# Orders of single instructions on every engine, with the rotary sine products and two decay products on GpSimd

## What is computed

```python
x = x + 0.5 * ffn0(layernorm(x))    # 8 experts, top 2, gated, and one shared expert
x = x + attn0(layernorm(x))         # 32 heads, no softmax: q (k v), then a group norm
x = x + 0.5 * ffn0(layernorm(x))
x = x + 0.5 * ffn1(layernorm(x))    # 8 experts, top 1, layernorm inside, gelu
x = x + attn1(layernorm(x))         # 8 heads, rotary q and k, gated running state
x = x + 0.5 * ffn1(layernorm(x))
```

```python
rope(x) = concat(x1 * c - x2 * s, x1 * s + x2 * c)      # x1, x2: halves of a head of 16
M = M * f_t + g_t * scale * (k_t outer v_t);  y_t = (q_t M) * o_t
```

## Time and profile before

| | us |
|---|---|
| median of three runs | 1223.96 (1218.2 to 1229.26) |
| span of the profiled execution | 1611.3 |
| PE busy in it | 1208.2 |
| DVE busy | 1037.9 |
| ACT busy | 881.7 |
| POOL busy | 645.2 |
| mean granted TensorE clock | 0.851 of full |

### The profile page before, as it was taken

One profiled execution on the slowest core, in us unless ns is written; L12 is line 12 of the kernel. 1 busy time (PEld: TensorE's weight loads), 2 busy tenths in 40 slices (PEclk: granted clock), 3 DMA queues, 4 the chain that ended last, 5 costly groups with the idle time before them and its releaser, 6 DMA issues.

```text
span 1611.3 us, 37336 instructions
## 1 busy us (share of the span) xinstructions
PE 1208.2 (75%) x14084; PEld 950.7 (59%) x14113; DVE 1037.9 (64%) x3441; ACT 881.7 (55%) x1505; POOL 645.2 (40%) x679
## 2 busy tenths in 40 slices
PE   3745767567766778767666766799989897989997
PEld 2423545455555666555554645677877676768776
DVE  7954655455645656666664664677767757888774
ACT  3545556334544445645543653676677445766764
POOL 1364443344555455555545453431322323342100
PEclk9876878787887978988887887898898978999989
DMA  8012323223132322222132222311210101010001
GB/s 263 14 50 62 79 68 75 59 63 83 57 84 70 78 71 76 62 65 55 57 87 67 68 67 66 76 43 46 56 46 23 28 18 33 15 29 24 2 9 34
DMA packets 172875, 93.77 MB, mean 58 GB/s; under 512 B 98516, under 2 KB 163183, under 8 KB 172575
## 3 DMA queue, kind: packets, MB, share of 16 engines
q1 hardware_dynamic: 115886, 35.64, 9.0%
q0 software_dynamic: 16384, 33.59, 7.3%
q10 hardware_dynamic: 40432, 22.17, 4.9%
HBM read 25.78 MB, written 45.61 MB: 44 GB/s over the span
## 4 chain that ended last, share of the span: by engine, by line
PE 37%; DVE 22%; ACT 13%; another core or an unknown queue 13%; issue 12%; POOL 1%; DMA 1%; ACTq 0%; POOLq 0%; DVEq 0%; SPq 0%
PE bank L759 8%; PE bank L581 3%; PE bank L820 2%; PE bank L967 2%; PE bank L806 2%; PE bank L839 2%; DVE x L1135 2%; PE bank L775 2%; PE sums L984 1%; PE sums L901 1%; PE bank L532 1%; PE sums L904 1%; ACT heads_store L1674 1%; DVE heads_store L1189 1%
## 5 line engine op out<-in xcount | busy, mean ns | idle before, releaser
L1914 POOL DMA_INDIRECT rows<-store,r_slot x256 | 258.8, 1011 | 185.1 <-DVE r_slot L1396 114.1
L759 PE MATMUL bank<-u_xp,w_hi 128*128 128x128 f16 x2432 | 267.3, 237 | 83.7 <-issue 74.0
L1930 POOL DMA_INDIRECT y_in<-ys,r_result x256 | 262.2, 1024 | 120.6 <-issue 70.3
L759 PE MATMUL bank<-u_xp,w_lo 128*128 128x128 f16 x1216 | 245.7, 237 | 34.6 <-issue 34.4
L759 PEld LDWEIGHTS bank<-u_xp,w_hi 128*128 x2432 | 212.3, 108 | 100.0 <-issue 94.4
L759 PEld LDWEIGHTS bank<-u_xp,w_lo 128*128 x1216 | 130.3, 107 | 47.1 <-issue 47.1
L581 PE MATMUL bank<-heads_store,w_hi 128*128 128x512 f16 x256 | 92.6, 449 | 7.0 <-DVE r_lg L1164 4.2
L1874 POOL TENSOR_SCALAR ve_last<-mv_last 128x4 f32<-128x4 f32 x16 | 3.1, 195 | 215.0 <-DVE mv_last L1092 214.9
L1698 ACT ACTIVATE heads_store<-bank,sc 128x512 f32<-128x512 f32 x64 | 43.3, 682 | 75.0 <-PE bank L581 41.1
L1135 DVE SCALAR_TENSOR_TENSOR x<-y_in,r_weight,x 128x128 f32<-128x128 f32 x256 | 72.5, 346 | 1.1
L1189 DVE TENSOR_TENSOR heads_store<-bank,heads_store 128x512 f32<-128x512 f32 x64 | 43.7, 686 | 42.7 <-ACT heads_store L1698 33.9
(11 more groups left out here) (434 smaller groups left out, 3478.4 us busy)
## 6 DMA issues: line engine op xcount, KB each, us to landing
ys<-u_y_even ACTq DMA_DIRECT2D x38, 256.0 KB
ys<-u_y_odd ACTq DMA_DIRECT2D x38, 256.0 KB
u_xp<-rows SPq DMA_TRANSPOSE x304
x<-x_dram SPq DMA_DIRECT2D x16, 256.0 KB, 5.6
rows<-store,r_slot POOLq DMA_INDIRECT x256
y_in<-ys,r_result POOLq DMA_INDIRECT x256
out_dram<-x SPq DMA_DIRECT2D x16, 256.0 KB
rows<-blank SPq DMA_DIRECT2D x48, 64.0 KB
```

What stands on the lines that cost most here:

```text
L759: ins = pe.matmul(B[:, of_block[j]], of_expert(wp, e, F16, part, which), xp_rows[:, xp, of_block[j]], start=(n == 0 and j == 0), stop=(n = ...
L1914: pool.indirect_dma_start(row_dram[g], bass.IndirectOffsetOnAxis(route.slot[g][:, i, t:t + 1].bitcast(U32), 0), rows[:, groups[g].first * ...
L1930: pool.indirect_dma_start(fetch.y[i][:, t, k, :], None, y_dram[g], bass.IndirectOffsetOnAxis(route.result[g][:, k, t0 + t:t0 + t + 1].bitc ...
```

## The change

Every engine's program becomes a generator that yields after each instruction (on PE: after each group of matmuls that ends in one signal). A letter now takes one such piece instead of a step:

```diff
-        def order(engine):
-            ahead = {which: iter(steps[which]) for which in steps}
-            return [next(ahead[which]) for which in turns[engine]]
+        def played(engine, visits):
+            lanes = {which: chain.from_iterable(visits[name](*what) for name, what in steps[which] if name in visits)
+                     for which in steps}
+            for which in turns[engine]:
+                next(lanes[which])
```

The five strings are replaced by longer ones (of DVE's, the first line before and after):

```diff
-                "yyyabcabcxabcxppywybbybaaryprpbprpbauppprbppbpcacrbcaapyabycabybccacrbycbabrcbararbaacrcayrrbbacrbcr"
+                "yyyyyyyyyyyyyyyyyyyyyyyyyayyxbxabyyyyyyycyyyyyyyyyypppppppppppybyyyyyyyyyyyyayyyyrrybaycypbrrrrrrrrr"
```

Where a run of instructions had one signal at its end, followed by a wait for it, each of them has its own now, so that the next can be placed between them:

```diff
                 for t in range(T):
-                    ins = dve.bn_stats(part[:, t, :], xc(c)[:, t, :])
-                mark(ins, "stats", *point)
-                on.wait_ge(*at("stats", *point))
+                    mark(dve.bn_stats(part[:, t, :], xc(c)[:, t, :]), "stats", *point, t)
+                    yield
                 for t in range(T):
+                    on.wait_ge(*at("stats", *point, t))
                     ins = dve.bn_aggr(mv[:, t, :], part[:, t, :])
```

The same is done in `weighed` and for the group norm's statistics. Row loads (SP) get a lane of their own, `z`, in the order of the units. One matmul without a reader, near PE's end (`warm`), is left out. In the second attention two kinds of product move from DVE to POOL, with the same shapes:

```diff
 # vector
-                    for hh in range(2):
-                        sinb = const["sin"][:, :, hh * hd:(hh + 1) * hd].unsqueeze(2).broadcast_to(
-                            [P, T, NHH, hd])
-                        ins = dve.tensor_tensor(per_head(rs)[:, :, :, hh * hd:(hh + 1) * hd],
-                                                per_head(s.qk)[:, :, :, (1 - hh) * hd:(2 - hh) * hd], sinb, ALU.mult)
-                    mark(ins, "rs", c)
-                    on.wait_ge(*at("rs", c))
-                    mark(dve.tensor_tensor(s.rc, s.rc, rs, ALU.add), "rc", c, "rope")
+                    mark(dve.tensor_tensor(per_head(s.rc), per_head(s.qk), cosb, ALU.mult), "cos", c)
+                    yield
+                    on.wait_ge(*at("cos", c))
+                    on.wait_ge(*s.by_pool.at("rs", c))
+                    mark(dve.tensor_tensor(s.rc, s.rc, s.rs[c % 2], ALU.add), "rc", c, "rope")
...
-                    dve.tensor_tensor(hv(s.qd), hv(s.qg[:, 1:T:2, :]), gates(s.ec[:, 1:T:2, :]), ALU.mult)
...
-                    dve.tensor_tensor(hv(s.kgs), hv(s.kg[:, 0:T:2, :]), gates(s.es[:, 0:T:2, :]), ALU.mult)
 # pool
+                if k == 3:
+                    on.wait_ge(*s.by_scalar.at("v", c, T - 1))
...
+                        ins = pool.tensor_tensor(per_head(s.rs[c % 2])[:, :, :, hh * hd:(hh + 1) * hd],
+                                                 per_head(s.qk)[:, :, :, (1 - hh) * hd:(2 - hh) * hd], sinb, ALU.mult)
...
+                elif k == 7:
+                    on.wait_ge(*s.by_scalar.at("es", c))
+                    on.wait_ge(*s.by_vector.at("qg", c))
+                    mark(pool.tensor_tensor(per_head(s.qd), per_head(s.qg[:, 1:T:2, :]), gates(s.ec[:, 1:T:2, :]),
+                                            ALU.mult), "qd", c)
+                    yield
+                    mark(pool.tensor_tensor(per_head(s.kgs), per_head(s.kg[:, 0:T:2, :]), gates(s.es[:, 0:T:2, :]),
+                                            ALU.mult), "kgs", c)
```

553 lines of the change are left out of this document (386 added, 167 removed).

## The result

The changed kernel takes 1300.95 us (median of 4 runs, 1292.96 to 1309.58), beside 1222.0 for the kernel before in the same comparison: a ratio of 1.064, 95% interval 1.057 to 1.071. It is slower. My forecast was 1190 us, and the range ended at 1240.

What follows compares the result with a forecast made beforehand. No single engine was taken to bound the kernel, but hand-offs between engines; 20 (DVE waits) + 12 (products) - 4 (standing) + 7 (finer order) = 35 us of 1219.8, against the median 1224 - 34 = 1190 us; range 1146 to 1240.

Steps and rivals of the forecast that it cites:

- The reading: Whole profile: "another core" and "issue", 391.5 of 1611.3 us, are mostly profiling; the sum stands against 1219.8 us of explained chain.
- what would break the reading most: Whole profile: the two unexplained entries are real time, so the chain shares by engine and the rate are off.
- finer order: All engines: short urgent instructions no longer wait behind whole steps; a twentieth of four waits' 141 us, 7 us gained.
- DVE terms: On DVE: 57 us of waits and 34 of products, less 12 of standing, times the rate.
- The rate: On DVE: 354 us of chain share out of 1037.9 us busy, 0.34 us of chain for each busy one.
- Waits inside DVE: On DVE: 479 fewer directly dependent instructions at 0.12 us each, 57 us of DVE, worth 20 us.
- Products off DVE: 32 sine and 32 decay products leave DVE: 34.1 us less busy, worth 12 us.
- their price on POOL: The moved products on POOL: 1.6 us for a sine and 0.8 for a decay product, 77 us in all.
- The standing at the sum: DVE waits for POOL's sine products at the rotary sum: 12 us in all, 4 us lost.
- rival 2: Rotary sum: DVE stands for POOL, sine products of 6 us each, 59 us lost, 1244 us; chance 0.13.
- the sign of less slack: Later stage: new waits of PE for ACT would mean that the order itself has less slack; no size given.

Runs made afterwards that it cites:

- before_third: The kernel before, unchanged, run again for a trace at the quick level: 1221.73 us, one run.
- old order: The kernel before's strings of whole steps, replayed with the changed kernel's single pieces and signals; with all products on DVE 1211.89 us, ratio 0.994 to the kernel before.
- fine order: The changed kernel's five engine strings; with all products on DVE 1299.35 us, ratio 1.064 to the kernel before at the quick level.
- fine_products_dve: The changed kernel with all four kinds of product back on DVE: 1691.6 us at the slow level, 1.048 of the kernel before.
- after_again: The changed kernel, unchanged, run again at the slow level: 1682.73 us, ratio 1.047 to the kernel before.
- fine_more_vector: The changed kernel with all products on DVE and eight added DVE instructions ahead of each chunk's cosine product: 1333.03 us, 1.091 of the kernel before.

## Why the prediction was wrong, step by step

**The reading.** The first step that failed is "these two entries are mostly what profiling adds, and make the sum against the 1219.8 us of explained chain". That the explained chain and the median agreed to 0.3% was chance. The two entries are real time on the chip of that trace: an unchanged copy took 1609.22 us there. I had named this as what would break the reading most, and it did: the waits of the earlier trace rows on which I built the gain of the finer order are small at the level of the median. In before_third:

```profile
ACT heads_store L1698 <- PE bank L581: 18.6, 18, 3.2
PE bank L556 <- ACT heads_store L1665: 11.9, 11, 3.1
DVE heads_store L1189 <- ACT heads_store L1698: 7.5, 5, 2.2
```

41.1, 31.4 and 33.9 us in the earlier trace rows are 18.6, 11.9 and 7.5 here, and the fourth, 34.6, is 5.7: 43.7 us in all instead of 141. PE is busy for 93% of the second attention (447.07 of 480), not for 88%, and DVE for 84%. But the right trace alone would not have saved the forecast. By the same method it gives a rate of 0.39 (33% of 1219.7, out of 1030.8), 31 us for the DVE terms, 2 for a twentieth of the waits and about 1190 us again. The steps below failed by themselves.

**The rate, 0.34 us for a busy one.** In the second attention 39.5 us more on DVE cost 51 us in the old order, a rate of 1.3, and 37.6 us cost 31 in the fine one, 0.8; in the first half the fine order's 18 us less on DVE brought nothing. An average over the chain is none of these.

**Waits inside DVE, 57 us, worth 20.** With the products on DVE in both, DVE is busy for 1030.8 us before and for 996.6 in the fine order: 34 us less, not 57, and 11 of the 34 are there in the whole order already (1019.7), which has the single signals alone. Worth: none that shows; the kernel with the fine order is 81 us slower. What the Trainium skill says of the drain (VectorE: DVE Perf Modes, section The DRAIN you can't avoid) would have given 0 for this term, which is nearer in effect, though busy time did fall.

**Products off DVE, 34.1 us, worth 12; their price on POOL.** The durations were near: 1315 ns for a sine product in the mean where I took 1600 (1183 in the median, closer to the estimate of 1.1 us), 899 and 828 for the decay products where I took 800:

```profile
L2116 POOL TENSOR_TENSOR store<-store,w_packed 128x512 f32<-128x512 f32 x32 | 41.5, 1315 | 40.0 <-ACT heads_store L1994 39.7
L2124 POOL TENSOR_TENSOR store<-store,heads_store 128x256 f32<-128x256 f32 x16 | 14.4, 899 | 101.0 <-ACT heads_store L2021 101.0
```

The standing at the sum was 7.1 us in the second attention where I took 12. But DVE's busy time fell by only 15 us through the move (996.6 to 981.9), not by 34, because other DVE instructions grew longer: 107 of them overlap a product on POOL, and these take 15.7 us more in all than by the median of the same instruction without one, which is most of the missing 19. Four normalising instructions that take 0.35 us each elsewhere take 2.92 us together. Two sine products start with the first of them; read one by one, the first two of the four take 1.27 and 1.21 us, each beside a sine product of 1.18 us, and the other two 0.33:

```profile
822.74 2.92 DVE L1142 TENSOR_SCALAR heads_store<-x,mv_last,rstd_last 128x128 f32<-128x128 f32 x4 [0.28 <-POOL rstd_last L2071]
```

```profile
822.74 2.32 POOL L2116 TENSOR_TENSOR store<-store,w_packed 128x512 f32<-128x512 f32 x2
```

And the 64x512 decay product on DVE, beside which I had called POOL's decay product free, is 860 ns long in the mean after (first row; 969 in the 10 that overlap a product on POOL, 679 in the 6 others) and 689 ns in fine_products_dve_2 (second):

```profile
L1756 DVE TENSOR_TENSOR store<-store,heads_store 64x512 f32<-64x512 f32 x16 | 13.8, 860 | 0.3
```

```profile
L1759 DVE TENSOR_TENSOR store<-store,heads_store 64x512 f32<-64x512 f32 x16 | 11.0, 689 | 0.2
```

I had this in the prediction as the Trainium skill's rule (SBUF — State Buffer, section Who interferes with whom), but for the cosine product alone, and left it out of the sum since no row showed it. It is there at the cosine product too, in 6 of the 16 chunks. In three of these DVE starts first and the sine product stands for it; in chunk 5 DVE then stands 2.28 us at the sum:

```profile
903.09 1.23 DVE L1705 TENSOR_TENSOR store<-store,w_packed 128x1024 f32<-128x1024 f32 x1 [0.69 <-ACT heads_store L1994]
906.60 1.22 DVE L1709 TENSOR_TENSOR store<-store 128x1024 f32<-128x1024 f32 x1 [2.28 <-POOL store L2116]
```

```profile
903.13 2.23 POOL L2116 TENSOR_TENSOR store<-store,w_packed 128x512 f32<-128x512 f32 x1 [1.37 <-ACT heads_store L1994]
```

That this is near my 2.0 us for such a chunk is luck: the products are shorter than I took them, and the block that I left out makes up for it. The worth of the move was none that shows in the fine order (1.064 with and without) instead of 12 - 4. In the old order it costs 3.9% (0.994 to 1.032): rival 2's mechanism is real, at sine products a third as long as the 4.2 us from which I let it decide. I had priced DVE's standing at 0.34, and had left out that POOL itself stands for ACT ahead of the decay products, 101.0 us, with norms behind it.

**Finer order, +7 us (ends -15 to +50).** This is the term that decided. It is -87 us, 1211.89 to 1299.35 with all else alike, and my lower end of -15 was a guess without a row. I had priced what a finer order lets pass, a twentieth of four waits, and put at nothing the waits that it makes. The sentence "an order with less slack loses when a duration is not what it assumed" named the direction; but the test for slack came out the other way (0.8 us for each added one in the fine order, 1.3 in the old one). What the runs show in its place: the same work on all engines, idle time up by 33 us on PE, 55 on ACT and 61 on DVE in the second attention, and a lower granted clock on top. PE's waits for ACT go from 6.8 to 29.9 us in it, the sign of less slack that I had named. Neither SP's old string nor a rearranged string of DVE gave the loss back, and two small rearrangements of the old order lost 2.0 and 2.7%.

**Open.** Which places of the strings lose it. No run has the old string of PE, ACT, DVE or POOL alone in the fine order. PE's string carries 1.3% when the others adapt; the remainder was not divided. Whether the strings lose because they were made for durations other than the chip's is not shown: an order from measured durations lost as well.

## What to carry to other kernels

Before a sum is made, see that the trace and the time come from the same level: take the span, not a part of the chain that happens to match, and ask for another trace where they differ. In this kernel's second attention, where PE and DVE are busy for 93% and 84%, the hand-made order is a net of hand-offs in which every engine's place depends on the others'. A microsecond added to DVE ahead of the cosine product cost 0.8 or 1.3 us there, not the 0.34 of its average share; microseconds taken from DVE in the first half brought nothing; and the orders that moved instructions into gaps lost time. So price a reordering by the waits that it can make as well as by those that it can remove, and run the new order without the other changes first. The one version at or below the kernel before came from changing less: the old order with the new signals and all products on DVE, 0.994 (0.991 to 0.996).

## What the hardware showed that I had not expected

**Two levels of one program.** At the slow level PE's instructions stand apart with nothing that they wait for. The largest wait of this kind in the changed kernel at the slow level (after_again), and then the largest at the quick one, where L788 has none:

```profile
PE bank L788 <- issue: 112.3, 120, 2.4
```

```profile
PE bank L918 <- issue: 2.1, 4, 1.3
```

The timeline of after_again shows it while POOL scatters rows to HBM, with scatter instructions at 173.41, 174.66 and 175.93 us:

```profile
173.07 0.22 PE L788 MATMUL bank<-u_xp,w_hi 128*128 128x128 f16 x1 [1.21 <-issue]
...
174.51 0.26 PE L788 MATMUL bank<-u_xp,w_hi 128*128 128x128 f16 x1 [1.17 <-issue]
175.93 0.27 PE L788 MATMUL bank<-u_xp,w_hi 128*128 128x128 f16 x1 [1.15 <-issue]
```

The mean granted clock is lower as well, 0.83 to 0.84 for the changed kernel there and 0.93 to 0.94 at the quick level. The cause was not tested, and no run tells whether it lies in the chip or in something else that ran on it. The difference falls mostly on the first half: the first cosine product of the changed kernel comes at 1040 us there and at 701 at the quick level, while its second attention takes 592 and 536 us.

**Standing and a lower clock come together.** At the quick level, each kernel whose PE idled more in the second attention also had a lower granted clock there: 0.97 for the two with 29 to 33 us of idle time, 0.93 for the four with 49 to 63, and 0.91 for fine_more_vector with 81 (566 - 484.55). PE is at 1.2 GHz for 27 us of the stretch in the kernel before and for 78 in the changed one.

**Side by side on SBUF.** Of the 192 L1142 instructions of the changed kernel, 13 run beside a product on POOL; they take 0.88 us in the mean and up to 1.54, the other 179 take 0.35. The cosine product has a median of 1218 ns with and without the products on POOL, since in 9 of the 16 chunks it starts when the sine products are through. In six of the others one of the two stands. In chunks 5, 6 and 7 it starts 0.04 to 0.06 us ahead of the first sine product, which then takes 2.21 to 2.23 us instead of 1.18; in chunks 4, 10 and 11 a sine product starts first, and the cosine product takes 1.46 to 1.64. The rule of the Trainium skill named above, of a DVE instruction with two SBUF inputs beside a GpSimd one that reads SBUF, says that such a pair excludes each other for a whole instruction; the trace agrees for the cosine product, with 2.23 us for 1.18. L1142 has one tensor input, and the trace shows the same for it, with 1.27 us beside a product of 1.18; no run shows by which way it comes to that.
